# Raw keys and values of masked attention computed in an early stage and kept in DRAM

## The reference, cut to what matters

```python
src_trans = jnp.einsum('bsf,of->bso', src, W_src) + b_src
tgt_trans = jnp.einsum('btf,of->bto', tgt, W_tgt) + b_tgt
src_trans = src_trans * src_mask[:, :, None]
tgt_trans = tgt_trans * tgt_mask[:, :, None]
src_key, src_val = jnp.split(src_trans, 2, axis=2)
...
scores = jnp.einsum('bthd,bshd->bhts', q, k) / np.sqrt(HEAD_DIM)
scores = jnp.where(src_mask[:, None, None, :] == 0, -jnp.inf, scores)
attn = jax.nn.softmax(scores, axis=-1)
tgt_update = jnp.einsum('bhts,bshd->bthd', attn, v).reshape(b, t, OUT_SIZE)
cat_tgt = jnp.concatenate([tgt, tgt_update], axis=2)
return jnp.einsum('btf,of->bto', cat_tgt, W_out) + b_out
```

## Time and profile before

| what | value |
|---|---|
| median of 3 runs | 3075.43 us |
| span of the profiled execution | 3070.0 us |
| own time of the profiled execution | not given apart; the runs lie 4 to 7 us above the span |
| TensorE busy | 2724.3 us, 89% of the span |
| VectorE, ScalarE, GpSimd busy | 53%, 47%, 46% |
| granted TensorE clock, mean | 0.942 of full |
| chain that ended last, share of TensorE | 55% |

### The profile page before, as it was taken

The page is one execution under the profiler, slowest core; times in us unless marked ns, Lnnn a source line. Parts: engine busy times, 40 slices in busy tenths (PEclk is TensorE's granted clock), DMA queues, the critical chain, the costliest instruction groups (busy, mean ns, idle before and its releaser), DMA issues.

```text
span 3070.0 us, 70943 instructions
## 1 busy us (share of the span) xinstructions
PE 2724.3 (89%) x25041; PEld 2119.4 (69%) x25041; DVE 1635.4 (53%) x3572; ACT 1435.2 (47%) x4582; POOL 1409.9 (46%) x1645
## 2 busy tenths in 40 slices
PE   7888988569899979969986889999996996999999
PEld 6777776446666656746655767787774665768888
DVE  7999999654356645551126753333333224556643
ACT  4666665444366657733327852222321335773310
POOL 3777777723466755543335652332322223663320
PEclk9999998779999999969997989999995998999999
DMA  3000000100000000141111020000016111010100
GB/s 99 3 2 2 2 2 2 55 30 1 23 15 17 14 20 1 55 146 43 45 64 47 0 94 11 7 10 10 7 54 220 33 32 52 1 48 29 53 10 20
DMA packets 75141, 106.09 MB, mean 35 GB/s; under 512 B 11024, under 2 KB 54672, under 8 KB 74656
## 3 DMA queue, kind: packets, MB, share of 16 engines
q1 hardware_dynamic: 68960, 86.68, 8.5%
q0 software_dynamic: 5952, 16.26, 1.7%
HBM read 88.50 MB, written 14.42 MB: 34 GB/s over the span
## 4 chain that ended last, share of the span: by engine, by line
PE 55%; POOL 4%; DVE 4%; ACT 3%; issue 3%; SPq 1%; DMA 1%; DVEq 0%; ACTq 0%; POOLq 0%
PE up_ps L2490 5%; PE e_out_ps L2508 5%; PE t_ps L664 4%; PE s_ps L650 3%; PE bank_a L1554 3%; PE bank_b L1554 3%; POOL probs L569 2%; PE up_ps L2484 2%; PE bank_a L612 2%; ACT probs L798 2%; PE bank_d L701 2%; PE frame_ps L1633 2%; PE bank_d L620 2%; PE bank_b L1570 2%; PE bank_a L1570 2%
## 5 line engine op out<-in xcount | busy, mean ns | idle before, releaser
L569 POOL TENSOR_TENSOR probs<-probs,inv 128x512 f32<-128x512 f32 x320 | 328.0, 1039 | 274.1 <-DVE inv L919 273.9
L3454 POOL TENSOR_TENSOR hc<-h,bc 128x1024 f32<-128x1024 f32 x128 | 302.0, 2360 | 112.5 <-DVE h L3735 86.4
L798 ACT ACTIVATE probs<-s_ps,negmax 128x128 f32<-128x128 f32 (+1 forms) x768 | 297.7, 415 | 6.4 <-DVE negmax L879 5.0
L3735 DVE TENSOR_TENSOR_SCAN h<-da,dbu_ps 128x1024 f32<-128x1024 f32 x128 | 292.5, 2286 | 11.1 <-DVE dbu_ps L3747 4.4
L664 PE MATMUL t_ps<-ident,probs 128*128 128x128 f32 x1280 | 208.2, 286 | 57.8 <-POOL probs L569 49.2
L664 PEld LDWEIGHTS t_ps<-ident,probs 128*128 128x128 f32 x1280 | 139.2, 141 | 124.7 <-POOL probs L569 59.4
L3682 ACT ACTIVATE da<-dta_ps 128x1016 f32<-128x1016 f32 x128 | 130.3, 1018 | 150.2 <-PE dta_ps L3544 149.9
L3544 PE MATMUL dta_ps<-dt,a_spread 32*128 32x128 f32 x2048 | 155.2, 291 | 43.1 <-ACT da L3682 23.0
L2414 POOL DMA_INDIRECT expert_rows_out<-y,row_to x62 | 61.1, 986 | 268.7 <-DVE y L2773 138.3
L879 DVE TENSOR_REDUCE negmax<-s_ps 128x4 f32<-128x1024 f32 (+1 forms) x128 | 156.6, 1223 | 44.7 <-PE s_ps L650 42.7
L3544 PEld LDWEIGHTS dta_ps<-dt,a_spread 32*128 32x128 f32 x2048 | 130.4, 194 | 67.2 <-ACT da L3682 30.0
(11 more groups left out here) (509 smaller groups left out, 6752.4 us busy)
## 6 DMA issues: line engine op xcount, KB each, us to landing
cT<-in_ctx_turned SPq DMA_DIRECT2D x32, 256.0 KB, 2.6
w_down<-in_L_ffn_w SPq DMA_DIRECT2D x8, 1024.0 KB, 12.3
w_up<-in_L_ffn_w SPq DMA_DIRECT2D x8, 1024.0 KB, 13.5
c_in<-in_ctx SPq DMA_DIRECT2D x16, 256.0 KB, 2.8
w_gate<-in_L_ffn_w SPq DMA_DIRECT2D x8, 512.0 KB, 6.8
w_up<-in_L_ffn_w SPq DMA_DIRECT2D x8, 512.0 KB, 9.0
w_down<-in_L_ffn_w SPq DMA_DIRECT2D x8, 512.0 KB, 9.0
w_gate<-expert_rows_out SPq DMA_DIRECT2D x8, 512.0 KB, 6.6
```

The costliest lines, as they stand in the source:

```text
L569: pool.tensor_tensor(probs[:, u % 2, i], probs[:, u % 2, i], inv[:, u % 2, HB * i:HB * (i + 1)].unsqueeze(2).broadcast_to([P, HB, W]), ALU ...
L798: last = act.activation(probs[:, u % 2, i, k, :], src, ACT.Exp, bias=negmax[:, u % 2, at], accum_out=sums[:, u % 2, at])
L3454: pool.tensor_tensor(hc[:, s % 4], h[:, s % 2], bc[:, j, 1, :].unsqueeze(1).broadcast_to([P, 2 * G, P]), ALU.mult).then_inc(hc_ready.sem, 1)
L3735: dve.tensor_tensor_scan(flat(h[:, s % 2]), flat(da[:, s % 4]), dbu_ps[s % 2][:, :, :, :].rearrange("p i g t -> p (i g t)"), 0.0, ALU.mult ...
```

## The change

The product of context and `w_src` is taken out of the masked stage and made in depool_ternary_stage, in pieces between its own TensorE work. ScalarE copies each item's 128 x 512 result to SBUF and issues its store to a DRAM tensor from its own queue. The masked stage loads these rows, two deep, and VectorE adds bias and mask from SBUF. TensorE's and VectorE's orders in the masked stage are written anew. Of the diff, the masked stage:

```diff
+            def load_raw(b):
+                sp.wait_ge(k_ready.sem, k_ready.done(b - 2))
+                sp.wait_ge(v_ready.sem, v_ready.done(b - 2))
+                sp.dma_start(raw[:, b % 2, :], kept.rows[b]).then_inc(landed[b % 2].sem, 16)
...
-                pe.wait_ge(v_ready.sem, v_ready.done(min(b + 3, B - 1)))
-                pe.wait_ge(out_used.sem, out_used.done(b - 1))
+                pe.wait_ge(out_used.sem, out_used.done(b - 2))
...
             for s in range(B + 2):
+                if 0 <= s - 1 < B:
+                    weigh(s - 1)
                 if s + 1 < B:
                     project_q(s + 1)
-                    project_k(s + 1)
+                if 0 <= s - 2 < B:
+                    out(s - 2)
                 if s < B:
                     turn_probs(s, 0)
-                if s + 1 < B:
-                    project_v(s + 1)
-                if s < B:
                     turn_probs(s, 1)
-                if 0 <= s - 1 < B:
-                    weigh(s - 1)
                 if s + 1 < B:
                     score(s + 1, 0)
                 if s + 2 < B:
                     turn_x(s + 2)
                 if s + 1 < B:
                     score(s + 1, 1)
-                if 0 <= s - 2 < B:
-                    out(s - 2)
...
             for s in range(B + 2):
+                if s < B:
+                    row_max(s)
                 if s + 1 < B:
-                    take(s + 1, q_made, xq_ps[:, 1], qT, bt, mrow_q, q_ready)
-                    take(s + 1, k_made, k_ps, kT, bk, mrow, k_ready)
-                    take_v(s + 1)
+                    take_k(s + 1)
+                    take_q(s + 1)
+                if 0 <= s - 2 < B:
+                    finish(s - 2)
                 if s < B:
                     copy_probs(s)
                 if 0 <= s - 1 < B:
                     normalise(s - 1)
                 if s + 1 < B:
-                    row_max(s + 1)
-                if 0 <= s - 2 < B:
-                    finish(s - 2)
+                    take_v(s + 1)
```

`k_ps` and the value half of `vo_ps` go, so that the result of `out` now has two halves, `out_ps`. The new `take_k` and `take_v` are the old ones with `raw` in SBUF in place of `k_ps` and `vo_ps`. The early stage, with the class that makes the pieces:

```diff
+class Ahead:
+    PARTS = 4
...
+    def load(self, eng, n):
+        eng.wait_ge(self.made.sem, self.made.done(n - 2))
+        eng.dma_start(self.cT[:, n % 2], self.context_turned[self.first + n]).then_inc(self.landed[n % 2].sem, 16)
+    def columns(self, pe, n, part, bank):
+        for cc in range(CC):
+            last = pe.matmul(bank[:, part * P:(part + 1) * P], self.w[:, cc, part * P:(part + 1) * P],
+                             self.cT[:, n % 2, cc, :], start=(cc == 0), stop=(cc == CC - 1))
+    def rows_of_values(self, pe, n, part, bank):
+        half = CC // 2
+        for cc in range(half * (part - 2), half * (part - 1)):
+            last = pe.matmul(bank[:, D:], self.cT[:, n % 2, cc, :], self.w[:, cc, D:], start=(cc == 0),
+                             stop=(cc == CC - 1))
...
+        if part == 0:
+            pe.wait_ge(self.landed[n % 2].sem, self.landed[n % 2].base + 16 * (n // 2 + 1))
+            pe.wait_ge(self.taken.sem, self.taken.done(n - 2))
...
+    def take(self, act, n, bank):
+        act.wait_ge(self.made.sem, self.made.done(n))
+        act.wait_ge(self.stored[n % 2].sem, self.stored[n % 2].base + 16 * (n // 2))
+        act.activation(self.staging[:, n % 2, :], bank, ACT.Copy).then_inc(self.taken.sem, 1)
+        act.wait_ge(self.taken.sem, self.taken.done(n))
+        act.dma_start(self.kept.rows[self.first + n], self.staging[:, n % 2, :]).then_inc(self.stored[n % 2].sem, 16)
...
+        parts_in_step = {s: 4 if s < 2 or s > PAIRS else 5 for s in range(1, PAIRS + 3)}
+        parts_in_step[1] = 0
+        parts_before_largest, parts_after_largest = 5, 4
...
+        first_late = parts_at(PAIRS + 2) + parts_before_largest + parts_after_largest
+        units_by_step = lambda s: parts_at(s) // Ahead.PARTS
+        units_by_item = lambda b: min(first_late + b, Ahead.PARTS * B) // Ahead.PARTS
...
             for s in range(1, PAIRS + 3):
+                late = 2 if s <= PAIRS else 0
                 if s <= PAIRS:
-                    products(2 * (s - 1))
+                    products(2 * (s - 1), max(parts_in_step[s] - late, 0))
                     products(2 * (s - 1) + 1)
                 if 1 < s < PAIRS:
                     turn_x(s)
+                make_ahead(min(late, parts_in_step[s]) if s <= PAIRS else parts_in_step[s])
                 if s >= 3:
                     turn_xn(s - 3)
+            make_ahead(parts_before_largest)
             pe.wait_ge(prep.sem, prep.done(1))
...
+            make_ahead(parts_after_largest)
             for b in range(B):
+                make_ahead(1 if b else 0)
                 product_ternary(b)
```

More of the change, by code:

```diff
@@ L1073, in sync @@
                 sp.dma_start(dst, src).then_inc(w_landed.sem, 16)
-            load_context(1)
-            for b in range(2, B):
-                sp.wait_ge(v_made.sem, v_made.done(b - 2))
-                load_context(b)
+            kept.wait(sp)
+            for b in range(B):
+                load_raw(b)
         def gpsimd(pool):
@@ L1212, in tensor @@
             project_q(0)
-            project_k(0)
             turn_x(1)
-            project_v(0)
             pe.wait_ge(loads.sem, first_in)
@@ L1270, in vector, with take_q, take_k @@
         def vector(dve):
-            def take(b, made, src, dst, bias, rows, ready):
-                dve.wait_ge(made.sem, made.done(b))
+            def take_q(b):
+                dve.wait_ge(q_made.sem, q_made.done(b))
                 dve.wait_ge(scored.sem, scored.done(b - 2))
                 for qc in range(DC):
-                    last = dve.scalar_tensor_tensor(out=dst[:, b % 2, qc, :], in0=src[:, qc, :], scalar=bias[:, qc:qc + 1],
-                                                    in1=rows[:, b, :], op0=ALU.add, op1=ALU.mult)
-                last.then_inc(ready.sem, 1)
+                    last = dve.scalar_tensor_tensor(out=qT[:, b % 2, qc, :], in0=xq_ps[:, 1, qc, :], scalar=bt[:, qc:qc + 1],
+                                                    in1=mrow_q[:, b, :], op0=ALU.add, op1=ALU.mult)
+                last.then_inc(q_ready.sem, 1)
+            def take_k(b):
+                dve.wait_ge(landed[b % 2].sem, landed_at(b))
+                dve.wait_ge(scored.sem, scored.done(b - 2))
+                for qc in range(DC):
+                    last = dve.scalar_tensor_tensor(out=kT[:, b % 2, qc, :], in0=raw[:, b % 2, qc * P:(qc + 1) * P],
+                                                    scalar=bk[:, qc:qc + 1], in1=mrow[:, b, :], op0=ALU.add, op1=ALU.mult)
+                last.then_inc(k_ready.sem, 1)
             def take_v(b):
-                dve.wait_ge(v_made.sem, v_made.done(b))
+                dve.wait_ge(landed[b % 2].sem, landed_at(b))
                 dve.wait_ge(bias_ready.sem, bias_ready.done(b))
                 dve.wait_ge(weighed.sem, weighed.done(b - 2))
-                dve.scalar_tensor_tensor(out=v[:, b % 2, :], in0=vo_ps[:, 0, :], scalar=mcol[:, b:b + 1],
+                dve.scalar_tensor_tensor(out=v[:, b % 2, :], in0=raw[:, b % 2, D:], scalar=mcol[:, b:b + 1],
                                          in1=bvm[:, b % 2, :], op0=ALU.mult, op1=ALU.add).then_inc(v_ready.sem, 1)
@@ L3025, in advance, with depool_ternary_stage @@
             n.advance(4)
[L3028 removed]
+def depool_ternary_stage(core, context, tables, context_turned, weights_ahead, kept, after=None):
     nc, loads = core.nc, core.weight_loads()
@@ L3075, in sync @@
                 sp.dma_start(c_in[:, b % 4, :], context[b]).then_inc(c_landed[b % 4].sem, 16)
+            ahead.load_weights(sp)
+            ahead.load(sp, 0)
+            ahead.load(sp, 1)
             for b in range(4, B):
@@ L3079, in sync @@
                 sp.dma_start(c_in[:, b % 4, :], context[b]).then_inc(c_landed[b % 4].sem, 16)
+                if b % 2 and b >= 7:
+                    ahead.load(sp, (b - 3) // 2)
+            for n in range(7, B):
+                ahead.load(sp, n)
         def gpsimd(pool):
@@ L3135, in turn_x, with make_ahead, products @@
                 last.then_inc(x_turned.sem, 1)
-            def products(b):
+            made = iter([(n, part) for n in range(B) for part in range(Ahead.PARTS)])
+            def make_ahead(parts):
+                for _, (n, part) in zip(range(parts), made):
+                    ahead.part(pe, n, part, bank_of(n))
+            def products(b, parts=0):
                 q, j = b // 2, b % 2
@@ L3143, in products @@
                               stop=(cc == DC - 1))
+                make_ahead(parts)
                 pe.wait_ge(u_ready.sem, u_ready.done(b))
@@ L3222, in save2, with keep_ahead @@
                                scale=rstd[:, 0, b:b + 1]).then_inc(x_saved.sem, 1)
+            def keep_ahead(units):
+                for n in range(keep_ahead.kept, units):
+                    ahead.take(act, n, bank_of(n))
+                keep_ahead.kept = max(units, keep_ahead.kept)
+            keep_ahead.kept = 0
```

(1 more changed line is left out.)

110 lines of the change are left out of this document (68 added, 42 removed).

## The result

| | before | after |
|---|---|---|
| median of 20 runs (lowest to highest) | 3075.3 us (3068.2 to 3082.0) | 3082.2 us (3073.0 to 3087.0) |
| profiled execution: time, span | time not given, 3070.0 us | 3082.1 us, 3080.4 us |
| ratio of the times | | 1.0019, 95% interval 1.0011 to 1.0027 |

The changed kernel is slower by 6 to 7 us, where 26.5 us less were forecast: 3082.2 us against 3049.

The account below looks back on a forecast made before the run. The prediction took TensorE to bound the masked stage and a chain between engines the early stage. Masked -36.0 us and early +9.5 us made -26.5 us, so 3075.4 us became 3049 us, bounds 3042 to 3063.

Parts of the forecast that it names:

- The masked stage, VectorE's part of the loop: Masked stage: VectorE's 4.37 us plus 3.0 us of exponentials, transposes and hand-overs set a 7.37 us loop.
- The forecast's own sign of being wrong: Wrong if early-stage steps grow over 8.5 us, or if the masked period is not within 7.3 to 7.9 us.
- the forecast of the stage: Masked stage: 14 periods of 7.5 us, +0.5 us at the end; -36.0 us in all, bounds -38.8 and -28.4.
- `take_k` and `take_v` from SBUF: Masked stage, VectorE: uncontended `take_v` costs nothing more, contended 0.46 us; a quarter taken, 0.13 us a period; `take_k` nothing.
- The rule of the Trainium skill: Masked stage, VectorE: half throughput would make the period 7.84 us and add 4.8 us, 3054; contended case 0.15 more.
- The end of the masked stage: Behind the last copy: `finish(14)` ahead of `normalise(15)` and perhaps a low TensorE clock; +0.5 us (0 to +2.5).
- The early stage: The projection's 64 parts placed there: +4.1 up to the maximum, +5.7 between halves, -0.3 after; +9.5 us, bounds +5 and +16.
- the +4.1 of the forecast: Early stage: transpose of the maximum at 630.1 in place of 625.95, with five parts before it.
- ScalarE's price of a unit: Early stage: a 0.6 us copy from PSUM, a wait of some 0.1 and a DMA issue (0.47): 1.2 us a unit.
- The wait at 635.96 and four parts at half clock: Early stage, between halves: first part waits for `taken(10)`; four parts take 3.5 us and 1.6 for the clock.
- "Slower": Whole kernel slower, chance 0.06; slow clock or unseen early-stage wait had 0.12, half beyond 3075; half clock throughout gave 3141.
- the range's lower bounds for the masked stage (-28.4): Masked stage at a 7.9 us period saves 28.4 us; with +16 for the early stage, -12.4, 3063.

Follow-up runs that it names:

- the filler: The changed kernel with 12 more transposes an item on TensorE, into an unused bank, where it waits for `aT`: 3067.9 us, ratio 0.9985 to the kernel before.
- the kernel with two buffers: The changed kernel with `o_ps` double-buffered, so `weigh` waits for `aT` of an item earlier: 3054.3 us, ratio 0.9947 to the kernel before.
- the two runs that take the wait out of the way: The changed kernel with `o_ps` double-buffered (3054.3 us), and the changed kernel with `project_q` ahead of `weigh` (3059.3 us); ratio 0.9947 each.
- the old order: The changed kernel with TensorE's and VectorE's masked-stage orders of before, without the two projections: 3084.5 us, ratio 1.0025 to the kernel before.

## Why the prediction was wrong

**The step that failed** is "The masked stage, VectorE's part of the loop": "The loop is 4.37 + 3.0 = 7.37 us. TensorE's 6.48 us fit in". I compared TensorE's busy time with that loop and took it that whatever is shorter fits. I had placed `out(s-2)` in time, but not `weigh(s-1)`, whose `wait_ge(a_ready ...)` stands unchanged in the code; before, this wait was a period old when `weigh` came, since `weigh` stood behind the transposes. In the new order `weigh` comes first, and the same wait asks for a value that VectorE has only just made. The loop then goes on through `out` and `finish`, which the forecast had both counted as slack. With that wait the loop is 8.04 us (the filler showed it alone), 0.67 us over the forecast's: 7.0 us of the stage between second and last copy against the kernel with two buffers. Another 15.6 us there are the clock, which falls after the 1.49 us gap, and 2.9 us the stage's end; I had priced a fall of the clock only at the stage's end and in the early stage. The forecast's own sign of being wrong, a masked period outside 7.3 to 7.9 us, came true: 8.04 to 9.7.

**Without that wait the forecast of the stage holds nearly:** 137.1 and 138.6 us in the two runs that take the wait out of the way, against 169.2 - 36.0 = 133.2 us. Period 7.30 us without contention (forecast 7.37), 7.45 to 7.6 with (forecast 7.5, bounds 7.3 and 7.9). The rest is at the start: item 0's copy stood 12.9 us behind the stage's first transpose in all kernels, 13.0 before, where the forecast took 1.7 us off; and the second copy came 8.3 us later, not 5.8.

**`take_k` and `take_v` from SBUF.** In the changed kernel `take_v` has a mean of 475 ns and `take_k` of 342 ns, against 484 and 346 ns with one input in PSUM. The rule of the Trainium skill that the prediction weighed ("Vector Engine (DVE) Microarchitecture Reference", "Points that are easy to get wrong": half throughput with two SBUF sources that are not bf16) is not borne out by these. The contention with GpSimd is real where `take_v` meets the residual: 701 ns on average in the run with two `o_ps`. The Trainium skill has it too ("GPSIMD Engine Reference", section 1, specifications: GpSimd shares its SBUF interfaces with VectorE instructions with two SBUF inputs), and here the trace agrees for the residual, but not for GpSimd's `b_v_masked`, beside which `take_v` took 470 ns.

**The end of the masked stage** was priced too low. The forecast took +0.5 us (0 to 2.5) from the earlier trace rows. In TensorE's timeline of the changed kernel:

```profile
2929.14 0.64 PE L1174 MATMUL o_ps<-pT,v 128*32 128x128 f32 x16 [3.27 <-DVE aT L1283]
...
2935.56 2.08 PE L1186 MATMUL out_ps<-w_out,xT 128*128 128x256 f32 x4 [3.41 <-DVE aT L1283]
```

From the last copy to the next stage's first transpose it is 13.7 us (2926.18 to 2939.86), before 10.6. The next stage then begins at the low clock (its first transposes 0.69 us, 0.44 before) and takes 140.5 us to the end of the span, against 137.5 before and in the two runs with `normalise` moved. But the run with the masked stage of before takes 139.0 us there too, its first transposes at 0.44 us and its first gate products at the low clock (4.4 us in place of 2.9). So at most some 1.5 us of the 3 can be laid to the changed end of the masked stage; the rest comes and goes without it.

**The early stage was right to 2 us:** +11.1 against +9.5 (bounds 5 and 16). Its steps keep their pace, as forecast: 7.77 us from one GpSimd root to the next, 7.76 before. Between stage start and the transpose of the maximum it is 79.04 us in place of 72.70, +6.3 against the +4.1 of the forecast. Most of the missing part is the wait of a unit for `taken(n-2)`, which I had priced only between the halves: four of them, 0.67 us once and 0.40 three times, 1.9 us in all. ScalarE's price of a unit was forecast at 1.2 us; its rows give 0.58 for the copy, and 0.33 to 0.35 for the DMA issue that I had taken at 0.47. The wait at 635.96 and four parts at half clock (5.26 us to the product at 641.22) came as forecast, 3.5 + 1.6 = 5.1.

**The rivals.** "Slower" had 0.06, bound to a half clock or an unseen wait in the early stage. The clock there was 0.94, and the cost as forecast. It was slower by a wait in the other stage, which had no rival at all: the range's lower bounds for the masked stage (-28.4) were those of one loop's terms, not of another loop. A range that holds the cases must ask which loops there are before it asks how long each is.

## What to carry to other kernels

When the order of an engine's steps is changed, list every wait of the moved step and work out how old the awaited value is in the new order; a single buffer's release that was a period old can become the newest value of the loop. Then walk every closed loop through the engines, GpSimd among them, and not only the longest of the old schedule: the two expectations that failed here, mine of the change and mine of the old order, each missed one. An order can be mended cheaply: moving one step of VectorE to where its result is not awaited gave 43 us, where the change around it had lost 6 to 7.

## What the runs showed of the chip beyond that

- One gap of 1.49 us on TensorE, in a period in which it is otherwise without idle time, was followed by a stretch at clock 0.50 in eight of twelve periods, and in four not; a gap of 1.22 us before them was, and one of 1.72 us after them too. The stretch measured was of 3 us. Half a microsecond of idle time an item, in gaps of up to 0.38 us, left it at 1.00. Filling the gap with useless transposes made the stage 14.1 us shorter.
- `take_v` with both inputs in SBUF takes 475 ns. Where GpSimd's addition of two SBUF tiles began before it, it takes 630 ns at 0.35 us of overlap and 780 ns at 0.51 us, and it ends 0.28 us behind the addition in both (2842.72 against 2842.44, 2850.32 against 2850.05). Where `take_v` began first, the addition at 2858.15, it takes 470 ns. Beside GpSimd's multiplication by a column, with one tile as input, it takes 470 ns too.
